# Starting values for the score banks from ScalarE and VectorE in place of an adding matmul, in a cross-attention on one core

## The reference, cut to what matters

```python
qp = (q @ w_qkvs.T); kp = (k @ w_qkvs.T); vp = (v @ w_qkvs.T)
scores = jnp.einsum('bqd,bkd->bqk', qh, kh) / temperature
attn = jax.nn.softmax(scores, axis=2)
out = jnp.einsum('bqk,bkd->bqd', attn, vh)
```

## Time and profile before

| | |
|---|---|
| runs of the kernel, median of 3 (lowest, highest) | 1595.29 us (1593.91, 1596.3) |
| profiled execution: its own time | 1597.26 us |
| its span | 1595.4 us |
| PE busy, share of the span | 94% |
| DVE, ACT, POOL busy | 67%, 45%, 36% |
| mean granted clock of PE | 0.983 of full speed |

### The profile page before, as it was taken

The page is one execution under the profiler, slowest core; times in us unless marked ns, Lnnn a source line. Parts: engine busy times, 40 slices in busy tenths (PEclk is TensorE's granted clock), DMA queues, the critical chain, the costliest instruction groups (busy, mean ns, idle before and its releaser), DMA issues.

```text
span 1595.4 us, 30310 instructions
## 1 busy us (share of the span) xinstructions
PE 1506.3 (94%) x11596; PEld 1014.9 (64%) x11596; DVE 1062.1 (67%) x2085; ACT 723.5 (45%) x1272; POOL 576.5 (36%) x632
## 2 busy tenths in 40 slices
PE   2889998999999799999999999999999999999998
PEld 2456765766666577777777777778885444444444
DVE  5855445565566567677868786855557875876766
ACT  2231122212121255565555565556666665465555
POOL 2220001000110567703370237001995664555655
PEclk9899999999999899999999999999999999999999
DMA  7431110110000368712360325000233442344443
GB/s 209 97 116 30 23 29 22 31 34 21 15 27 27 69 137 171 182 19 62 61 160 6 62 61 130 10 19 2 74 97 103 120 142 89 119 139 126 143 128 109
DMA packets 143773, 128.43 MB, mean 81 GB/s; under 512 B 86837, under 2 KB 124173, under 8 KB 142605
## 3 DMA queue, kind: packets, MB, share of 16 engines
q1 hardware_dynamic: 127053, 110.62, 27.2%
q0 software_dynamic: 2272, 12.06, 2.5%
q10 hardware_dynamic: 14304, 3.81, 1.1%
HBM read 106.21 MB, written 5.28 MB: 70 GB/s over the span
## 4 chain that ended last, share of the span: by engine, by line
PE 80%; DVE 11%; ACT 3%; DMA 3%; POOL 2%; issue 2%; SPq 0%; DVEq 0%; POOLq 0%; ACTq 0%
PE ps L1723 5%; PE ps L1725 5%; PE ps L1724 5%; PE ps L1928 4%; PE ps L2001 4%; PE ps L2002 4%; PE ps L2003 4%; PE ps L1922 4%; PE ps L1923 4%; PE ps L1896 4%; PE ps L1885 4%; PE ps L1891 4%; PE ps L1886 4%; PE ps L1861 3%; PE ps L2013 2%; PE ps L2015 2%
## 5 line engine op out<-in xcount | busy, mean ns | idle before, releaser
L989 ACT ACTIVATE region_c<-ps 128x720 f16<-128x720 f32 (+1 forms) x228 | 175.6, 770 | 258.2 <-PE ps L1896 258.1
L857 POOL TENSOR_TENSOR region_k<-region_c,region_k 128x480 f16<-128x480 f32 x198 | 217.0, 1098 | 170.7 <-ACT region_k L1110 170.6
L1359 DVE TENSOR_TENSOR region_c<-ps,region_c 128x720 f16<-128x720 f32 (+1 forms) x228 | 206.1, 904 | 95.4 <-ACT ps L990 93.1
L1723 PE MATMUL ps<-region_k 128*128 128x360 f16 (+1 forms) x752 | 241.2, 321 | 5.5 <-DVE region_k L1183 4.3
L1725 PE MATMUL ps<-region_k 128*128 128x360 f16 (+1 forms) x752 | 240.8, 320 | 0.0
L1724 PE MATMUL ps<-region_k 128*128 128x360 f16 (+1 forms) x752 | 240.6, 320 | 0.0
L1364 DVE TENSOR_REDUCE region_c<-ps 120x1 f32<-120x512 f32 x252 | 173.6, 689 | 85.9 <-PE ps L1861 83.5
L1922 PE MATMUL ps<-region_k,region_c 128*120 128x129 f16 (+1 forms) x1368 | 180.8, 221 | 0.0
L1923 PE MATMUL ps<-region_k,region_c 128*120 128x128 f16 (+1 forms) x1368 | 180.0, 220 | 0.0
L990 ACT ACTIVATE ps<-ps 128x720 f32<-128x720 f32 (+1 forms) x228 | 174.4, 765 | 0.0
L741 POOL TENSOR_TENSOR vare<-mv,eps 120x6 f32<-120x6 f32 x20 | 4.0, 199 | 464.9 <-DVE mv L1262 464.9
(11 more groups left out here) (277 smaller groups left out, 2821.1 us busy)
## 6 DMA issues: line engine op xcount, KB each, us to landing
gates<-gates_dram SPq DMA_DIRECT2D x384, 120.0 KB, 2.8
region_c<-in_k SPq DMA_DIRECT2D x56, 256.0 KB, 2.9
region_c<-in_v SPq DMA_DIRECT2D x56, 256.0 KB, 3.1
region_c<-in_WcT POOLq DMA_DIRECT2D x8, 1024.0 KB, 7.0
region_c<-in_experts SPq DMA_DIRECT2D x18, 352.0 KB, 3.1
gates<-band_dram SPq DMA_DIRECT2D x26, 189.0 KB
region_c<-in_k POOLq DMA_DIRECT2D x14, 256.0 KB, 3.0
region_k<-region_c SPq DMA_TRANSPOSE x120, 3.1
```

What stands on the lines that cost most here:

```text
L857: g.tensor_tensor(a_lo[u], ac[u], a_hi[u], ALU.subtract).then_inc(s["a_lo_ready"], 1)
L1359: v.tensor_tensor(halves(p_lo[u][0:parts]), two(2 * u, parts), halves(p_hi[u][0:parts]), ALU.subtract).then_inc(s["lo_ready"], 1)
L1723: mm(o, wh[:, m, j], xh[:, j:j + w], start=(j == 0), stop=False)
```

## The change

The matmul that adds the negated maxima (L1896) goes for most tiles. In its place the negated maxima are written into the score bank first, and the three product matmuls accumulate on them (`start=False`).

- For w=1, tiles 2 to 55 of every batch: ACT copies 360 columns from a float16 table in SBUF (`shiftb`, the negated maxima spread over all partitions) into the bank, behind the two exponentials of the tile before (`seed`).
- For w=0, tiles 4 to 55 of the last batch: DVE copies 360 columns into the bank, behind the low part two tiles before.
- At the start of each batch PE makes the spread table for w=1 in bank 4 with one matmul, and ACT copies it into SBUF between the two exponentials of tile 0. In the last batch the same is done for w=0 behind the first exponential of tile 1.
- In `key_scores` the order is now all of w=0, then all of w=1; the wait for a seed stands ahead of the first matmul of its w. The matmul for a maximum stands behind the second matmul of w=0 (before: behind the fourth of the tile). The first maximum of a batch and the maxima of the tail move behind the scores of tile 1.

```diff
+SEED_BOTH = 4
+        shiftb = w2_sb[:].rearrange("p m c -> p (m c)").bitcast(F16)[:, 0:T]
+        def act_seeds(b, t):
+            return (KT - 2) * b + t - 1
+        def dve_seeds(t):
+            return t - SEED_BOTH + 1
...
                 a.activation(halves(p_hi[u][0:parts]), st, ACT.Exp).then_inc(s["p_hi_ready"], 1)
+                if t == 0:
+                    spread_shift(b, 1)
+                if t == 1 and b + 1 == B:
+                    spread_shift(b, 0)
                 a.activation(st, st, ACT.Exp).then_inc(s["exp_sum"], 1)
+                if 1 <= t < KT - 1:
+                    seed(b, t + 1, 1 - u)
+
+            def spread_shift(b, w):
+                act.wait_ge(s["shift_ps"], b + 2 - w)
+                if w == 1 and b:
+                    act.wait_ge(s["seed_act"], act_seeds(b, 1))
+                a.activation(shiftb[:, w * HALF:(w + 1) * HALF], bank(4)[:, 0:HALF], ACT.Copy
+                             ).then_inc(s["shift_sb"], 1)
+
+            def seed(b, t, u):
+                if t == 2:
+                    act.wait_ge(s["shift_sb"], b + 1)
+                act.wait_ge(s["lo_ready"], TILES * b + t - 1)
+                a.activation(bank(2 * u + 1)[:, 0:HALF], shiftb[:, HALF:T], ACT.Copy).then_inc(s["seed_act"], 1)
...
                 v.tensor_tensor(halves(p_lo[u][0:parts]), two(2 * u, parts), halves(p_hi[u][0:parts]),
                                 ALU.subtract).then_inc(s["lo_ready"], 1)
+                if b + 1 == B and SEED_BOTH <= t + 2 < KT:
+                    if t + 2 == SEED_BOTH:
+                        dve.wait_ge(s["shift_sb"], B + 1)
+                    dve.wait_ge(s["lo_ready"], TILES * b + t + 1)
+                    v.tensor_copy(bank(2 * u)[:, 0:HALF], shiftb[:, 0:HALF]).then_inc(s["seed_dve"], 1)
...
                 for w in range(2):
                     q = slice(w * HALF, (w + 1) * HALF)
-                    mm(bank(2 * u + w, parts)[:, 0:HALF], kh, q_hi[:, b, q], start=True, stop=False)
-                    mm(bank(2 * u + w, parts)[:, 0:HALF], kh, q_lo[:, b, q], start=False, stop=False)
-                if row is not None:
-                    maximum_of(b + 1, *row)
-                for w in range(2):
-                    q = slice(w * HALF, (w + 1) * HALF)
-                    mm(bank(2 * u + w, parts)[:, 0:HALF], kl, q_hi[:, b, q], start=False, stop=False)
-                if isinstance(t, int) and t == 0:
-                    pe.wait_ge(s["shift_ready"], b + 1)
+                    o = bank(2 * u + w, parts)[:, 0:HALF]
+                    seeded = 2 <= t < KT if w else b + 1 == B and SEED_BOTH <= t < KT
+                    if seeded and w:
+                        pe.wait_ge(s["seed_act"], act_seeds(b, t))
+                    elif seeded:
+                        pe.wait_ge(s["seed_dve"], dve_seeds(t))
+                    mm(o, kh, q_hi[:, b, q], start=not seeded, stop=False, skip_group_check=True)
+                    mm(o, kh, q_lo[:, b, q], start=False, stop=False, skip_group_check=True)
+                    if w == 0 and row is not None:
+                        maximum_of(b + 1, *row)
+                    last = mm(o, kl, q_hi[:, b, q], start=False, stop=seeded, skip_group_check=True)
+                    if not seeded:
+                        if t == 0:
+                            pe.wait_ge(s["shift_ready"], b + 1)
+                        last = mm(o, ones16[0:P, 0:parts], sh[:, q], start=False, stop=True, skip_group_check=True)
+                last.then_inc(s["st_ps"], 1)
+
+            def spread_shift(b, w):
                 sh = (shift[b % 2] if b else shift0[:]).rearrange("p r q -> p (r q)")
-                for w in range(2):
-                    last = mm(bank(2 * u + w, parts)[:, 0:HALF], ones16[0:P, 0:parts],
-                              sh[:, w * HALF:(w + 1) * HALF], start=False, stop=True)
-                last.then_inc(s["st_ps"], 1)
+                mm(bank(4)[:, 0:HALF], ones16[0:P, :], sh[:, w * HALF:(w + 1) * HALF], start=True, stop=True
+                   ).then_inc(s["shift_ps"], 1)
...
-                if b + 1 < B:
-                    prepare_tail(b + 1)
+                spread_shift(b, 1)
...
-                            key_scores(b, 8 * i + t + 1, (t + 1) % 2, row=early)
+                            key_scores(b, 8 * i + t + 1, (t + 1) % 2, row=early if i or t else None)
+                        if i == t == 0:
+                            pe.wait_ge(s["shift_sb"], b + 1)
+                            if b + 1 < B:
+                                prepare_tail(b + 1)
+                                maximum_of(b + 1, *first)
+                            else:
+                                spread_shift(b, 0)
```

More of the change, by code:

```diff
@@ L500, in tower @@
             post_full post_free k16_in k16_ready first_ps first_free klo_ready v_split mx_ps mx_free shift_ready
-            st_ps p_hi_ready exp_sum lo_ready pv_done acc_ps acc_free rden_ready wf_done
+            shift_ps shift_sb seed_act seed_dve st_ps p_hi_ready exp_sum lo_ready pv_done acc_ps acc_free rden_ready wf_done
             shifted_logits logits_exp msk_ready gates_ready gate_turned gates_out
@@ L1882, in key_scores @@
                 kh, kl = k_hi[b % 2][:, at], k_lo[b % 2][:, at]
+                sh = (shift[b % 2] if b else shift0[:]).rearrange("p r q -> p (r q)")
                 for w in range(2):
                     q = slice(w * HALF, (w + 1) * HALF)
-                    mm(bank(2 * u + w, parts)[:, 0:HALF], kh, q_hi[:, b, q], start=True, stop=False)
-                    mm(bank(2 * u + w, parts)[:, 0:HALF], kh, q_lo[:, b, q], start=False, stop=False)
-                if row is not None:
-                    maximum_of(b + 1, *row)
```

## The result

The changed kernel takes 1605.22 us (median of 7, 1602.77 to 1606.5) against 1593.91 us for the kernel before in the same comparison (median of 7, 1588.49 to 1597.69). The ratio is 1.0069, 95% interval 1.0051 to 1.0087: slower by 11 us. The forecast was 1604 us. The two profiled executions lie 9.2 us apart (1606.5 and 1597.26 us).

The account below looks back on a forecast made before the run. PE set the pace before; a 2.58 us ring through ACT's seed would after. Terms +0.8, -9.7, +14.2, -1.7, +3.8, +1.6 gave +9.0 on 1597.3, 1606; median 2.0 lower: 1604 us. Range 1589 to 1621.

Parts of the forecast that it names:

- The ring: Once per tile, ACT's exponentials and seed and PE's w=1 matmuls wait for each other; 2.58 us.
- Short tiles of the last batch: 48 last-batch intervals up to 2.72 us, mean 2.284, lengthen to 2.58 us: +14.2 us.
- Norms in the ring: Norms on ACT behind a seed delay the next exponential, 0.3 us over the ring; 12 of 18 groups count: +3.8 us.
- Short tiles of batches 0 to 2: 97 intervals up to 2.72 us, mean 2.572, go to 2.58 us, the whole saving eaten: +0.8 us.
- Long tiles: Intervals of 2.75 us and more, PE still setting the pace: 65 in batches 0 to 2, -9.7 us; 6 in last, -1.7.
- Starts of the batches: ACT's copy of the spread between tile 0's exponentials delays the second and the low part: 4 x 0.4 = +1.6 us.
- a sign of being wrong: Prediction wrong if last-batch exponentials stay under 2.45 us apart, PE's clock under 0.9, or PE idles at DVE's seed or maxima.
- Costed at nothing: DVE's last-batch seeds, taken as 0.5 us with 0.4 to spare, ACT's wait for the low part, and the moved maximum: no cost.
- The earlier place of the maximum: Maximum matmul, moved ahead of two matmuls, asks for bank 4 0.3 us earlier; PE waits for the seed anyway: no cost.
- The short ring: Rival: PE starts when ACT's next instruction could, ring 2.415 us, total 1584 us; chance 0.15 with a clear gain.
- PE as pace setter: Rival: the wait for seeds is met in time, -41 + 1 us, total 1555 us; chance 0.04.
- The clock: Rival: PE's idling in last-batch tiles drops it to 1.2 GHz, 70 us, total 1674 us; chance 0.03.

Follow-up runs that it names:

- last_batch_copy_nobody_waits_for: last_batch_unseeded plus, in the last batch, an ACT copy of 360 columns into unused SBUF that no engine waits for; 1592.1 us, ratio 1.001.
- last_batch_act_seed_only: Changed kernel, but DVE seeds nothing: w=0 of the last batch adds its maxima by matmul, ACT still seeds; 1606.5 us, ratio 1.009.
- changed_with_own_bank: Changed kernel with the spread of the maxima in bank 5 and the maxima in their old places; 1606.91 us, ratio 1.0092.
- seed_between_maximum_first: seed_between_exponentials, but DVE reads the first maximum of an even tile ahead of the low part; 1597.24 us, ratio 1.0029.
- seed_between_own_bank: seed_between_maximum_first with the spread of the maxima through bank 5 besides; 1594.91 us, ratio 1.0014.
- last_batch_unseeded: Changed kernel with seeds only in batches 0 to 2; the last batch adds maxima by matmul in both banks; 1591.02 us, ratio 0.9992.
- seed_between_exponentials: Changed kernel with ACT's seed between the two exponentials in batches 0 to 2 and DVE's seeds alone in the last; 1605.45 us, ratio 1.0092.
- seeds_by_table: Changed kernel, seeding in batches 0 to 2 only tiles with earlier intervals of 2.6 us or more; last batch DVE's seeds alone; 1591.24 us, ratio 0.9988.

## Why the prediction was right, point by point

- *The ring.* Right in place and in members: PE waits for ACT's seed, ACT for the third w=1 matmul. Removing the last batch's seeds takes the loss away, the same work without the wait costs nothing in tiles without steps, and a second copy in the wait adds its length to every tile. Forecast 2.58 us, measured 2.54: the seed takes 0.46 us, not 0.50. The 0.69 to its start, the 0.06 to PE and the 0.355 to the exponential came as taken from the rows.
- *Short tiles of the last batch.* +14.2 forecast for 48; +14.25 measured over the 47 of them behind tile 2, norms included. With the ring at 2.54 the term is +12.3, and what follows adds the rest.
- *Norms in the ring.* Right: an interval with a norm is 2.87 to 2.90 us in the last batch, 0.35 over the ring, and the 1.73 us that won it back before is now 2.52. Forecast 0.3 each. The 2.90 itself is ACT's own work and not the ring's, for last_batch_copy_nobody_waits_for has it too; the ring's part is the 2.52 in place of 1.73.
- *Short tiles of batches 0 to 2.* +0.8 forecast; +0.1 measured over 94, norms included: the ring eats the saving, as worked out. At 2.54 us the 97 would give -3.1; the norms take that back.
- *Long tiles.* -9.7 and -1.7 forecast, -8.6 and -1.9 measured. The three tiles of the router are among them and account for -1.8 in all (24.18 us before, 22.42 after), which follows the clock more than the change.
- *Starts of the batches.* The term that was mis-sized: +1.6 forecast, +3.7 measured. The interval from tile 1 to 2 is 4.06 us in batches 0 to 2, where it had 2.46. I had priced ACT's copy and overlooked that the tail's maxima and the first maximum, moved behind the scores of tile 1, form a chain over bank 4:

```profile
894.48 0.46 PE L1909 MATMUL ps<-region_k,region_b 128*120 128x32 f16 x6
894.97 0.36 DVE L1418 TENSOR_REDUCE region_c<-ps 120x6 f32<-120x192 f32 x1 [2.41 <-PE ps L1909]
895.25 0.90 DVE L1394 TENSOR_TENSOR region_c<-ps,region_c 128x720 f16<-128x720 f32 x1
895.48 0.40 PE L1902 MATMUL ps<-region_k,region_b 128*120 128x512 f16 x1 [0.54 <-DVE region_c L1418]
896.06 0.68 DVE L1405 TENSOR_REDUCE region_c<-ps 120x1 f32<-120x512 f32 x1
896.89 0.40 PE L1902 MATMUL ps<-region_k,region_b 128*120 128x512 f16 x1 [0.34 <-DVE region_c L1405]
```

DVE has waited 2.41 us for the tail, with the low part of tile 0 queued behind it, and each maximum waits for the reading of the one before. Here, and only at these starts, PE idles at the maxima, which the prediction had named as a sign of being wrong. The kernels with the spread in bank 5 take 1.5 us off this interval and give 0.9 back one tile earlier. Of the +3.7, -0.9 is the first interval of batch 0 (12.02 to 11.16 us); kernels with the same code there show 11.16 to 12.22, so that part may be scatter.

- *Sum.* The terms as measured: 14.25 + 0.1 - 8.6 - 1.9 + 3.7 and 0.4 at the tails give +8.0, the 8.1 us between first and last exponential; 1.5 us ahead of the stage are not the change's. The forecast's +9.0 came out of a ring 0.04 us too long over 145 tiles (5.8 us) and of starts (2.1), long tiles (0.9), tails (0.4) and norms (some 1.4, what is left over) that were too cheap. They cancelled in part, and that the total came so close is luck. So is the agreement within 1 us of the medians: the kernel before had 1595.29 us in the runs that the forecast started from, 1593.91 over all seven, and 1589.91 to 1594.85 in the later groups. The medians are 11.3 us apart, the traces show 8.1 us in the stage (9.8 without the router's tiles), and what makes up the rest of the 11.3 is not shown.
- *Costed at nothing.* DVE's seeds take 0.54 us (0.5 taken) and PE never waits for them in the last batch's stretch: right, and last_batch_act_seed_only shows it. The earlier place of the maximum shows no cost but at the starts; no run tests it by itself.
- *Rivals.* The short ring needed PE to start ahead of the seed's reported end; it started 0.06 us behind. PE as pace setter fell with 2.54 us a tile. The clock stayed at 0.99 in the last batch although PE idled 14% of it; that rival is out for the pauses that the ring makes. It is not out for the starts of the batches: there PE's granted clock fell to about half for some microseconds in four of the thirteen traces (batch 1 in changed_with_own_bank, seed_between_maximum_first and seed_between_own_bank, batch 3 in last_batch_unseeded), and the profiled execution of the changed kernel had 1.00 there.

## What to carry to other kernels

When work moves from the busiest engine to an idle one, follow what the busiest then waits for, and whether that wait stands behind something that waits for the busiest itself. Add up the ring once around from the rows; it is the pace, whatever the busy shares are, and work on the new engine can be free only outside of it, and where that engine has idle time left. Then look for the next chain of nearly the same length: here the way over a PSUM bank that PE writes and DVE reads came to 5.12 us a pair against 5.13. Apart from the kernels with ACT's seeds in the last batch and seed_between_exponentials, all versions ended within 0.3% of the start.

## What the runs showed of the hardware

A copy of 360 columns from float16 in SBUF takes ACT 0.46 us into PSUM and 0.49 us into SBUF, against 0.47 us from PSUM: the 0.03 us that I had added for an SBUF source is 0.02 with an SBUF target and does not show with a PSUM target. The same copy as the seed takes DVE 0.54 us.

The tile with the router's small matmuls in batches 1 to 3 lasts from 6.2 to 8.9 us in the 39 cases of the thirteen traces, with PE's granted clock between 1.00 and 0.71. At 1.00 it is 6.2 to 6.6 us, at 0.73 and less 8.3 to 8.9. Here it is for batch 2 in the changed kernel and in seeds_by_table (columns as above):

```profile
977.54:986.11 8.57, 8.57 (x51) 6.44 (x49) 2.58 (x4) 1.82 (x4) 6.17 (x9) 0.73 0.88 154
```

```profile
976.60:983.18 6.58, 6.58 (x51) 5.22 (x49) 3.28 (x4) 1.82 (x4) 3.82 (x6) 1.00 0.93 175
```

The same 51 matmuls of PE took 2 us more at the lower mean clock. What PE did before the clock fell in the changed kernel was work without a pause, a run of float32 matmuls of 64 columns (L1878, L1879); from 981.44 us on they stand 0.29 us apart where it was 0.175. It is not this change: last_batch_act_seed_only, whose code in that batch is the changed kernel's, has 6.58 us at 1.00. The three tiles together last 20.6 to 24.2 us over the traces, and so differences of a few us between totals, or between stretches with that tile in them, tell little.
